# Two pair layers on one core: the first chunk's residual ahead of a sum folding, and four gates ahead of the first square root

## The reference

```
x   = layernorm(pair) * w + b
left  = sigmoid(x @ left1) * (x @ left2);  right = sigmoid(x @ right1) * (x @ right2)
p   = einsum('nsre,nkre->nske', left, right)
p   = layernorm(p) * w2 + b2                      # the "second norm"
g   = sigmoid(x @ gate)
x1  = pair + (p @ out_w) * g                      # the residual
```

## Time and profile before

| | |
|---|---|
| median of 3 runs | 122.13 us (121.76 to 123.0) |
| the profiled execution | 122.19 us |
| its span in the trace | 120.4 us |
| PE busy | 94.3 us (78%) |
| DVE busy | 88.2 us (73%) |
| ACT busy | 73.6 us (61%) |
| POOL busy | 69.6 us (58%) |
| DMA | 4.51 MB, mean 37 GB/s |

### The profile page before, as it was taken

The page is one execution under the profiler, slowest core; times in us unless marked ns, Lnnn a source line. Parts: engine busy times, 40 slices in busy tenths (PEclk is TensorE's granted clock), DMA queues, the critical chain, the costliest instruction groups (busy, mean ns, idle before and its releaser), DMA issues.

```text
span 120.4 us, 1797 instructions
## 1 busy us (share of the span) xinstructions
PE 94.3 (78%) x566; PEld 72.0 (60%) x566; DVE 88.2 (73%) x221; ACT 73.6 (61%) x129; POOL 69.6 (58%) x82
## 2 busy tenths in 40 slices
PE   1954799279779969999584999999999999696000
PEld 1943345167557759965231669888798889596000
DVE  1069999399999890776999635677498989799920
ACT  2245462886997537996138964555997798861100
POOL 5046688706099200884650597957835787995800
PEclk9997555958999999999998599999999999999755
DMA  2799990000000000000000000000000005429796
GB/s 43 140 138 153 147 142 8 0 0 0 5 0 0 0 3 5 0 3 0 0 0 0 0 0 5 0 0 3 0 0 5 0 0 87 75 34 144 109 145 103
DMA packets 33484, 4.51 MB, mean 37 GB/s; under 512 B 33348, under 2 KB 33476, under 8 KB 33476
## 3 DMA queue, kind: packets, MB, share of 16 engines
q1 hardware_dynamic: 32160, 4.06, 26.1%
q10 hardware_dynamic: 1316, 0.35, 1.5%
HBM read 2.31 MB, written 2.10 MB: 37 GB/s over the span
## 4 chain that ended last, share of the span: by engine, by line
PE 38%; DVE 35%; ACT 7%; issue 6%; DMA 5%; POOL 3%; SPq 0%; DVEq 0%; POOLq 0%
DVE lr L614 6%; PE bank L965 6%; PE bank L1008 6%; PE bank L875 5%; DMA x_tok<-in_x 5%; PE bank L1017 4%; DVE sums L585 4%; PE bank L979 3%; POOL acc_q L348 3%; PE bank L982 3%; PE bank L980 3%; DVE sums L570 3%; PE bank L938 3%; DVE lr L794 3%; DVE st L593 2%
## 5 line engine op out<-in xcount | busy, mean ns | idle before, releaser
L875 PE MATMUL bank<-lr_blk,xnT 64*128 64x256 f32 x128 | 21.2, 470 | 5.6 <-DVE lr L614 4.0
L875 PEld LDWEIGHTS bank<-lr_blk,xnT 64*128 64x128 f32 x128 | 14.4, 228 | 9.9 <-ACT xnT L426 5.2
L364 POOL TENSOR_TENSOR x_low<-x1T,x_high 128x512 fp32r<-128x512 f32 x8 | 11.0, 1380 | 12.1 <-ACT x_high L497 12.1
L614 DVE TENSOR_TENSOR lr<-bank,sig_lr 128x512 f32<-128x512 f32 x16 | 15.8, 1041 | 2.6 <-ACT sig_lr L436 2.3
L415 ACT ACTIVATE std<-st,eps 128x16 f32<-128x16 f32 (+4 forms) x14 | 4.4, 317 | 13.0 <-DVE st L600 5.9
L280 POOL TENSOR_TENSOR xc<-x_tok,sums 128x512 f32<-128x512 f32 (+2 forms) x7 | 8.0, 1144 | 7.4 <-DVE sums L578 7.4
L356 POOL TENSOR_TENSOR t_tok<-p_sb,rstd 128x512 f32<-128x512 f32 x7 | 10.4, 1491 | 2.8 <-DVE rstd L751 2.8
L436 ACT ACTIVATE sig_lr<-bank 128x512 f32<-128x512 f32 x16 | 9.4, 598 | 4.0 <-PE bank L875 3.9
L380 POOL TENSOR_TENSOR sq<-lr,row_rep 128x512 f32<-128x512 f32 x7 | 9.8, 1401 | 2.0 <-DVE lr L797 2.0
L965 PE MATMUL bank<-tT,out_blk 128*128 128x512 f32 x16 | 8.9, 638 | 2.2 <-DVE x1T L768 2.2
L372 POOL TENSOR_TENSOR oT<-o_a,rsum 128x512 f32<-128x512 f32 x8 | 8.7, 1090 | 2.5 <-issue 1.9
(11 more groups left out here) (119 smaller groups left out, 236.1 us busy)
## 6 DMA issues: line engine op xcount, KB each, us to landing
x_tok<-in_x SPq DMA_DIRECT2D x14, 128.0 KB, 4.3
out<-sq SPq DMA_DIRECT2D x7, 256.0 KB, 3.3
x_tok<-in_x SPq DMA_DIRECT2D x4, 64.0 KB, 4.6
w_rep<-in_weights ACTq DMA_DIRECT2D x1, 180.5 KB
out<-sq ACTq DMA_DIRECT2D x1, 128.0 KB, 4.5
out<-sq SPq DMA_DIRECT2D x1, 128.0 KB, 4.9
row_rep<-in_rows ACTq DMA_DIRECT2D x1, 32.0 KB, 5.1
```

The lines of the kernel that those rows point to most:

```text
L364: nc.gpsimd.tensor_tensor(x1_low[:, c % 2], x1T[:, c % 3], x1_high[:, c % 2], ALU.subtract).then_inc(x1_low_ready, 1)
L614: nc.vector.tensor_tensor(lr[:, :, s].rearrange("p f s -> p s f"), src[:, :, 2 * CH:4 * CH], sig_lr[:, j % 3].rearrange("p (s f) -> p s f" ...
L875: last = nc.tensor.matmul(dst, xnT[half, c, k * P:(k + 1) * P], lr_blk[half].rearrange("p g m c -> p g (m c)"), start=True, stop=True, ski ...
```

## The change

Three edits to the order, none to what is computed.

On VectorE `variance2(rest, 8)`, the folding for the later 80 tokens, stood in front of the chunk loop. Now it stands in the loop at i = 1, behind `residual0(0)`. The reciprocal of the rest, which stood behind `residual0(0)` at i = 1, now stands behind `residual0(1)` at i = 2.

On ScalarE four gates (chunks 0 to 3) instead of two come out in front of the first root, so that one (chunk 4) instead of three follows the second root at i = 1. At i = 1 `high1(0)` and `evacuate_tT(2)` now stand in front of the wait for the second `var2`, its root and the gate behind it; before, `high1(0)` came behind the gates and `evacuate_tT(2)` at i = 2.

TensorE, GpSimd and the DMA queues keep their order.

```diff
-GATES_FIRST = 2
+GATES_FIRST = 4
...
             for i in range(CHUNKS + 3):
-                if i < CHUNKS:
+                if i < CHUNKS and i != 2:
                     evacuate_tT(i)
                 if i == 1:
+
+                    high1(0)
+                    evacuate_tT(2)
                     act.wait_ge(var2, 2)
                     root(1, FIRST2, P, root2)
                     for c in range(GATES_FIRST, 5):
...
-                if 0 <= i - 1 < CHUNKS:
+                if 1 <= i - 1 < CHUNKS:
                     high1(i - 1)
...
-            variance2(rest, 8)
...
                 if 0 <= i - 1 < CHUNKS:
                     residual0(i - 1)
                 if i == 1:
+                    variance2(rest, 8)
+                if i == 2:
                     dve.wait_ge(root2, 2)
                     nc.vector.reciprocal(rstd[:, 1, rest], std[:, 1, rest]).then_inc(rstd2, 1)
```

## The result

The changed kernel took **126.76 us** in the median of four runs (125.58 to 128.26), against 122.28 (four runs, 121.76 to 123.0): slower, ratio 1.0276, 95% interval 1.0183 to 1.0369. The profiled execution took 125.82, 3.63 more than the profiled one before. Repeated later beside 17 runs of the kernel before, the same kernel took 126.17 (six runs, 125.62 to 127.52), ratio 1.0339, interval 1.0294 to 1.0384.

What follows compares the result with a forecast made beforehand. TensorE's third turn of the loop was taken to bound the kernel, so a later L of chunk 0 moves the end one for one. L +2.04 and slow clock +1.70 on the profiled 122.19 gave 125.9 us, range 123.8 to 127.0.

Steps and rivals of the forecast that it cites:

- Step 1: ScalarE: two more gates before the first root make that root start 0.31 us later.
- Step 2: VectorE: u of chunk 0 starts 1.07 us earlier, at 62.53; TensorE's next product starts at 63.82.
- Step 3: VectorE's folding in its new place: 2.30 us alone plus 1.20 held by GpSimd's x1_low, 3.50 in all.
- T: The end of VectorE's folding for the later tokens, forecast at 67.9, bounds 66.71 and 68.97.
- Step 4: ScalarE behind the folding: root, load and four gates put L of chunk 0 at 71.7, 2.04 us later.
- Step 5: TensorE's clock falls with or after the stand before L; the 3.4 us slow stretch loses 1.7 us.
- late recovery: TensorE's clock behind the stand: up to 2.5 us lost; chance 0.09 together with a longer hold.
- Sum: At the kernel's end: +2.04 for L later and +1.70 for the slow stretch, +3.74 us in all.
- two rivals on the clock: TensorE's stand before L costs no clock: 123.0 with the folding free (chance 0.08), 124.2 with the hold (0.10).
- no turn-taking: VectorE's folding is not held by x1_low: L at 70.51, +2.55 us, 124.7; chance 0.16.
- the clock recovers in time: TensorE's stand before L: folding free, no clock loss, L 0.85 later, 123.0, within 1%; chance 0.08.
- faster: x1 of chunk 0 sets the pipeline and the gates are hidden; 1.07 alone gives 121.1; chance 0.05.

Runs made afterwards that it cites:

- e3: Changed kernel, but GpSimd's first x1_low also waits for the end of the folding: 125.55 us, ratio 1.0271.
- e4: Changed kernel with four idle products in TensorE's stand between G and L of chunk 0: 124.21 us, ratio 1.0146.
- e10: Changed kernel with GpSimd's first x1_low waiting for the folding and two idle products between G and L of chunk 0: 123.53 us, ratio 1.0095.
- e5: Changed kernel with no gate behind the second root and gate 7's product one turn earlier on TensorE: 126.84 us, ratio 1.0389.
- e2: Kernel before with VectorE's two moves alone, ScalarE in its old order: 127.76 us median of four, no ratio.
- e1: Kernel before with four gates instead of two in front of the first root, nothing else: 122.39 us, ratio 0.9997.
- e6: Kernel before with e5's order on ScalarE and TensorE, three gates before the first root, the folding cut in two: 123.48 us, ratio 1.0117.
- e9: e6 plus two idle products in TensorE's stand before chunk 3's transposes, and gate1(0) in front of high1(1): 121.81 us, ratio 0.9970.
- e7: Kernel before with four gates before the first root and gate 7's product in TensorE's stand before the second q: 121.52 us, ratio 0.9952.

## Why the prediction was right

The forecast of 125.9 rested on a sum of 3.74 against the profiled execution; 3.63 was measured between profiled executions, and the median lies 0.9 above the forecast and inside the range. Point by point:

- *Step 1, the first root 0.31 later.* Right: the root starts at 57.51, 0.53 behind A, where it started 0.23 behind A before. The load took 1.28 and the root followed 0.02 behind it; there was no further drain.
- *Step 2, u at 62.53, q of chunk 1 at 63.82, a stand of 0.8.* Measured 62.47, 63.76 and 0.85.
- *Step 3, 2.30 for the folding alone and 1.20 for one hold, T = 67.9.* Measured 3.43 (64.34 to 67.77), with one held instruction, the fourth, and T = 67.77. Without x1_low beside it 2.33 (e3), and the hold moves L by 1.10 (e3) and G1 by 1.11 (e4 against e10).
- *Step 4, L at T + 3.80.* Measured 3.83. From A, L is 2.06 later than before; the sum had 2.04. e5 shows that the gates and nothing else kept L.
- *Step 5, 1.7 us of clock on top.* Measured 1.64 (changed kernel against e4). The size held some luck. The prediction took over the 3.4 us that the slow stretch had lasted before. The two profiles of the changed kernel have 3.4 as well, but in e2 and e5 it lasted 6.8, with 2.3 and 2.4 us lost (e5 had 4.8 us of work in it), just inside the bound of 2.5 for a late recovery. In e3 it began 0.5 before the end of the stand and cost 1.3.
- *Sum.* In A to G1: 0.96 bare + 1.11 hold + 1.64 clock = 3.71 (16.13 to 19.84). TensorE-bound behind it, right to 0.02 us.

The two rivals on the clock took the length of the stand to decide (1.41 full, 2.17 not). That is too simple: behind 2.18 in e1 the clock stayed full. Behind the 4.4 us here it fell in both profiles of the changed kernel.

The rival "no turn-taking" falls with L732's 1.34, "the clock recovers in time" with the 75.3, and "faster" with e2 and e5: with an early x1 of chunk 0, first the gates, then the normalising of chunk 3 hang on the folding that was pushed back. What the prediction left out is the spread: it added its sum to one profiled execution, and the medians of the changed kernel lie 0.94 and 0.55 above its two profiled ones. The loss behind the stand was 1.6 in both of these; where the longer runs lost more has no trace.

Where I was wrong is the sizing in later runs. In e5 and e6 I had found the next wait (3.8 and 1.9 us of stand) and not asked what it does to the clock; e9 gave less than expected, since GpSimd's product came late in the next turn; and the times of e2 and e10 lie 0.4 and 0.2 above their ranges, that of e3 0.8 above its +2.5.

## What to carry to other kernels

Moving a block behind the step that the bottleneck engine waits for helps only if nothing else hangs on the block: list every engine that waits for it (here a root, a table load, four gates and a normalising) before looking at what comes earlier. A stand of TensorE has two prices, its length and the slow work behind it; work put into the stand takes away the second (e4). In e7, where the work is useful and due soon, it cost nothing (A to G1 15.31, against 15.29 in e1), though its own share of the 0.6 us is not shown. And where VectorE and GpSimd both read two inputs from SBUF, look up which GpSimd instruction a moved block will lie beside, since here even an 80-element addition waited for a whole one (1.34 us for 0.23).

## What the runs showed of the hardware that was not expected

The granted clock goes with differences between runs of one and the same kernel that are larger than many changes are worth. In the first phase, which is the same code in all kernels here, the profile of the changed kernel has the clock at half from about 24.1 to 27.5; that of e1 has it at half from 23.4 to 30.2, and reaches A 1.13 us later. First the changed kernel, then e1 (length of the window, busy of PE, PEld, DVE, ACT and POOL, then PEclk):

```profile
27.50:28.00 0.50, 0.50 (x6) 0.17 (x3) 0.50 (x5) 0.00 (x0) 0.04 (x1) 0.96 0.00 0
```

```profile
27.50:28.00 0.50, 0.50 (x4) 0.05 (x2) 0.50 (x6) 0.00 (x0) 0.23 (x1) 0.50 0.00 0
...
30.00:30.50 0.50, 0.50 (x8) 0.40 (x6) 0.26 (x3) 0.14 (x1) 0.00 (x0) 0.78 0.00 0
```

All twelve profiles fall in these two groups: the six in which the slow stretch there lasts 3.4 us have A between 56.79 and 57.16, the six in which it lasts 6.8 between 57.59 and 58.36. A slow clock need not cost time: the changed kernel has it at half from 10.5 to 20.7 as well, e4 does not, and they reach A at 56.98 and 57.00. So a mean clock says little by itself, 0.900 for the one and 0.965 for the other.

The two long runs of the changed kernel (127.71 and 128.26) had mean granted clocks of 0.877 and 0.878, the short ones 0.900. By these means and the spans that is some 6 us more at half clock (an estimate), enough for the 2.0 to 2.6 us that they are longer; where it lay no trace shows.

The clock fell behind stands of 1.91 (e6), 2.17 (before), 3.83 (e2) and 4.43 us, and inside those of 1.85 (e3) and 3.79 (e5). It stayed full behind 1.31 (e7) and, in e1's profile, behind 2.18; so the same length of stand goes either way. That filling a stand makes the times steady is not shown: e4 has all four runs within 0.16 us, but e10, whose stand is filled too, has ten runs that spread over 1.9 us.
